# TensorE reads the normalised columns themselves, and SyncE reads two tile places at its block's start

## What is computed

```python
def _L1_ffn_ref(x, ln1_w, ln1_b, w_qkv, w_proj, ln2_w, ln2_b, gate_w, gate_b, w1, w2):
    ...
    x = x + _msa(_layernorm(x, ln1_w, ln1_b), w_qkv, w_proj)     # 16 heads of 8 columns, softmax attention within a batch
    x = x + _moe_mlp(_layernorm(x, ln2_w, ln2_b), gate_w, gate_b, w1, w2)   # each row goes to 1 of 8 experts, 128 -> 512 -> 128
    return x
```

## Time and profile before

| | |
|---|---|
| runs | 586.36 to 586.48 us, median 586.46 |
| profiled execution | 586.56 us, its span 584.8 us |
| mean granted TensorE clock | 0.944 |
| busy: TensorE, VectorE, ScalarE, GpSimd | 504.4, 357.7, 283.5, 152.5 us |
| attention block | 375.8 to 496.2 us of the span |
| expert block | 496.3 us to the end |

### The profile page before, as it was taken

One profiled execution on the slowest core, in us unless ns is written; L12 is line 12 of the kernel. 1 busy time (PEld: TensorE's weight loads), 2 busy tenths in 40 slices (PEclk: granted clock), 3 DMA queues, 4 the chain that ended last, 5 costly groups with the idle time before them and its releaser, 6 DMA issues. The chain is left out here.

```text
span 584.8 us, 33765 instructions
## 1 busy us (share of the span) xinstructions
PE 504.4 (86%) x14446; PEld 411.1 (70%) x14446; DVE 357.7 (61%) x1202; ACT 283.5 (48%) x691; POOL 152.5 (26%) x270
## 2 busy tenths in 40 slices
PE   0799999999996999899999979689999970799995
PEld 0688888888885654566666658468888850799994
DVE  4655555555556666566666446557999985355552
ACT  4222222221221694455555544558887851577772
POOL 2111111111110000000000017543467665155553
PEclk9899999999998999999999998669999995799998
DMA  8060000000000027494230002000011112333430
GB/s 272 23 233 1 0 0 0 0 0 0 0 0 2 0 41 162 132 321 75 73 92 0 2 2 76 1 4 1 0 58 39 58 66 91 80 111 101 111 106 18
DMA packets 22653, 34.36 MB, mean 59 GB/s; under 512 B 3616, under 2 KB 15909, under 8 KB 22216
## 3 DMA queue, kind: packets, MB, share of 16 engines
q1 hardware_dynamic: 19824, 27.23, 16.8%
q0 software_dynamic: 2784, 6.56, 3.2%
HBM read 25.98 MB, written 8.26 MB: 59 GB/s over the span
## 5 line engine op out<-in xcount | busy, mean ns | idle before, releaser
L231 PEld LDWEIGHTS ps_u<-v_cur,buf_b 128*32 128x32 f32 x7936 | 78.6, 110 | 12.1 <-DVE v_cur L300 9.4
L231 PE MATMUL ps_u<-v_cur,buf_b 128*32 128x32 f32 x7936 | 82.5, 198 | 3.7 <-DVE buf_b L289 2.4
L215 PE MATMUL ps_v<-buf_a,u_pad 128*32 128x128 f32 x1984 | 68.5, 280 | 7.5 <-issue 6.1
L215 PEld LDWEIGHTS ps_v<-buf_a,u_pad 128*32 128x32 f32 x1984 | 53.1, 112 | 11.1 <-issue 9.4
L300 DVE RECIPROCAL v_cur<-ps_vt 128x32 f32<-128x32 f32 x124 | 35.3, 327 | 32.3 <-PE ps_vt L222 32.3
L593 PE MATMUL ps_h<-buf_c,up 128*128 128x512 f32 x96 | 50.8, 626 | 0.4 <-DVE buf_c L809 0.2
L1735 POOL DMA_INDIRECT out<-yb,token_i x39 | 38.4, 984 | 48.2 <-DVE resid L1837 47.1
L179 POOL TENSOR_TENSOR u_hist<-inv_u,r_sum 128x16 f32 x62 | 13.8, 223 | 132.2 <-DVE inv_u L307 132.2
L985 POOL MEMSET eps<- 128x1 f32 x1 | 0.1, 99 | 166.4 <-POOLq L526 166.4
L1758 PE MATMUL m_h<-xT,w_near 128*128 128x128 f32 x312 | 43.0, 283 | 0.0
L195 ACT ACTIVATE over<-u_diff 128x32 f32<-128x32 f32 x31 | 7.1, 230 | 72.4 <-POOL u_diff L175 72.4
(11 more groups left out here) (309 smaller groups left out, 1133.8 us busy)
## 6 DMA issues: line engine op xcount, KB each, us to landing
cw_b<-cw_d SPq DMA_DIRECT2D x16, 512.0 KB, 8.1
xt<-sorted_x SPq DMA_DIRECT2D x39, 136.0 KB
w<-in_w SPq DMA_DIRECT2D x2, 2048.0 KB, 16.4
buf_a<-in_x SPq DMA_DIRECT2D x4, 512.0 KB, 6.4
buf_b<-in_x_t SPq DMA_DIRECT2D x4, 512.0 KB, 6.8
buf_d<-in_x_nt SPq DMA_DIRECT2D x1, 2048.0 KB, 9.9
sorted_x<-nobody SPq DMA_DIRECT2D x1, 1088.0 KB, 4.6
out<-yb,token_i POOLq DMA_INDIRECT x39
```

Of the source, the lines that this page charges most:

```text
L215: last = mm(ps_v[h][32 * j:32 * j + 32, 0:D], u_pad[:, h, j, 32 * i4:32 * i4 + 32], K[:, g * D:(g + 1) * D], start=i4 == 0, stop=i4 == TI - 1)
L231: last = mm(rows_u[h][32 * q:32 * q + 32, g, :], KT[:, b * N:(b + 1) * N], v_cur[:, h, k:k + 1].broadcast_to([P, WIDE]), start=True, stop= ...
```

## The change

The buffers `xs`, their copies and the semaphore `x_in` go. TensorE's three projection matmuls of a chunk read `xn_t`; within the loop their operand's address is worked out from the loop's register. In the expert block SyncE reads the places of tiles 0 and 1 before its two waits, and from the third tile on it reads as before.

```diff
-        xs = mem.sb("xs", [P, 2, CB, N])
...
-                g.tensor_copy(xs[:, 0], xn_t[:, 0:CB, :]).then_inc(x_in, 1)
-
...
-                def chunk_in(k):
-                    if k >= 2:
-                        pool.wait_ge(v_mm, k - 1)
-                    g.tensor_copy(xs[:, k % 2], xn_t[:, k * CB:(k + 1) * CB, :]).then_inc(x_in, 1)
-
-                chunk_in(1)
...
-                    if c + 2 < NC:
-                        chunk_in(c + 2)
...
-                def project(c, k):
-                    pe.wait_ge(x_in, c + 1)
+                def batches_of(c):
+                    return xn_t[:, c * CB:(c + 1) * CB, :] if isinstance(c, int) else xn_t[:, bass.ds(c * CB, CB), :]
+
+                def project(c):
                     if past(c, 1):
                         pe.wait_ge(qk_out, c)
-                    mm(ps_qk[:, 0, :], w_qkv[:, 0, :], xs[:, k], start=True, stop=True)
-                    mm(ps_qk[:, 1, :], w_qkv[:, 1, :], xs[:, k], start=True, stop=True).then_inc(qk_mm, 1)
+                    mm(ps_qk[:, 0, :], w_qkv[:, 0, :], batches_of(c), start=True, stop=True)
+                    mm(ps_qk[:, 1, :], w_qkv[:, 1, :], batches_of(c), start=True, stop=True).then_inc(qk_mm, 1)
...
-                    mm(ps_v[:, 0:CT], w_qkv[:, 2, :], xs[:, k], start=True, stop=True).then_inc(v_mm, 1)
+                    mm(ps_v[:, 0:CT], w_qkv[:, 2, :], batches_of(c), start=True, stop=True).then_inc(v_mm, 1)
...
             def _(sp):
+                first = [sp.value_load(tables.base_i[0:1, d:d + 1], min_val=0, max_val=SLOTS - P) for d in range(2)]
                 sp.wait_ge(tables.sent, 16 * N)
                 sp.wait_ge(tables.filled, 16)
                 for d in range(TILES):
                     k = d % BUFS
-                    at = sp.value_load(tables.base_i[0:1, d:d + 1], min_val=0, max_val=SLOTS - P)
+                    at = first[d] if d < 2 else sp.value_load(tables.base_i[0:1, d:d + 1], min_val=0, max_val=SLOTS - P)
```

More of the change, by code:

```diff
@@ L1269, in attend_and_route @@
         names = ("qk_mm", "v_mm", "s_mm", "t_mm", "o_mm", "ot_mm", "p_mm", "r_mm",
-                 "qk_out", "exp_done", "t_out", "ot_out", "x_in", "rooted", "act_own",
+                 "qk_out", "exp_done", "t_out", "ot_out", "rooted", "act_own",
                  "max_done", "sub_done", "v_out", "on_done", "x2_done", "summed", "row_ends", "hot_done", "slots_done",
                  "own", "heads", "v_read", "scoring")
-        (qk_mm, v_mm, s_mm, t_mm, o_mm, ot_mm, p_mm, r_mm, qk_out, exp_done, t_out, ot_out, x_in,
+        (qk_mm, v_mm, s_mm, t_mm, o_mm, ot_mm, p_mm, r_mm, qk_out, exp_done, t_out, ot_out,
          rooted, act_own, max_done, sub_done, v_out, on_done, x2_done, summed, row_ends, hot_done, slots_done,
@@ L1335, in past, with values @@
                     return not isinstance(c, int) or c >= n
-                def project(c, k):
-                    pe.wait_ge(x_in, c + 1)
+                def batches_of(c):
+                    return xn_t[:, c * CB:(c + 1) * CB, :] if isinstance(c, int) else xn_t[:, bass.ds(c * CB, CB), :]
+                def project(c):
                     if past(c, 1):
                         pe.wait_ge(qk_out, c)
-                    mm(ps_qk[:, 0, :], w_qkv[:, 0, :], xs[:, k], start=True, stop=True)
-                    mm(ps_qk[:, 1, :], w_qkv[:, 1, :], xs[:, k], start=True, stop=True).then_inc(qk_mm, 1)
-                def values(c, k):
+                    mm(ps_qk[:, 0, :], w_qkv[:, 0, :], batches_of(c), start=True, stop=True)
+                    mm(ps_qk[:, 1, :], w_qkv[:, 1, :], batches_of(c), start=True, stop=True).then_inc(qk_mm, 1)
+                def values(c):
                     if past(c, 1):
@@ L1433, in body @@
                     if not isinstance(c, int) or c + 1 < NC:
-                        project(c + 1, 1 - k)
-                        values(c + 1, 1 - k)
+                        project(c + 1)
+                        values(c + 1)
                     if past(c, 2):
@@ L1442, in _ @@
                 pe.wait_ge(made, RANKS)
-                project(0, 0)
-                values(0, 0)
+                project(0)
+                values(0)
                 body(0, 0, 0)
```

## The result

The changed kernel takes 580.93 us (median of 15 executions, 578.75 to 584.10), the kernel before 584.89 (15 executions beside them, 581.80 to 586.73). The ratio is **0.9937 [0.9918, 0.9956]**: faster by 0.6%, where the forecast was 586.1 and "no change that can be told". The same kernel on two other chips gave 0.9951 [0.9923, 0.9979] and 0.9937 [0.9911, 0.9963]. The profiled execution after is 579.32 us, its span 577.6 and its mean granted clock 0.957; before it was 586.56, 584.8 and 0.944.

The account below looks back on a forecast made before the run. Bounds: GpSimd's copy at the start, VectorE in late pairs, GpSimd's sends at the tail, TensorE in the experts. 0.21 + 0.71 less 0.26 leaves 0.66, half kept: 586.46 - 0.33 = 586.1 us; range 585.0 to 587.3.

Parts of the forecast that it names:

- The first copy goes: -0.21: Start of the attention block: TensorE starts 0.42 us earlier without GpSimd's copy of chunk 0, of which 0.21 us stays.
- The halving: Attention start: if the clock's rise keeps its time, 0.42 us more of low clock does the work of 0.21.
- The odd chunks' collisions: -0.71: Late loop pairs: copies slow VectorE's L1602 by 0.24 us, for which TensorE waits; three such copies go, 0.71 us less.
- rival C: No effect: collisions are coincidence, the start is bound by fetching, SyncE's 0.26 is halved; 586.6 us, chance 0.14.
- GpSimd's sends also slow VectorE a little; they stay: Late pairs, L1590: a slowdown put down to GpSimd's sends, which the change keeps, so no gain was counted.
- The even chunks: 0: Late pairs: 0.18 us freed at L1582 is lost as VectorE's reciprocal waits for TensorE's mixing; 0, at most 0.56.
- TensorE's operand: 0: Loop projections: register operations for the address are covered by the sequencer's lead of 0.9 to 1.2 us; bounds 0 and 7.2.
- rival B: Slower: address registers in the loop's three projection calls per chunk starve the array; up to 591.7 us, chance 0.10.
- SyncE: +0.26: Hand-over to the experts: the second read now delays tile 0's DMA, first expert matmul 0.26 us later; bounds -0.1, +0.7.
- Half is kept in the experts: -0.33: Experts' start: 0.66 us earlier, but at half speed up to a clock rise that keeps its time, so 0.33 remains.
- Rival A: More is kept: the even chunks' 0.56 counts too, the rises move with the work, nothing halved; 585.0 us, chance 0.18.
- Its neighbour at 585.8: Between forecast and 585.0: the clock's rises move, the even chunks give nothing; counted with the forecast, together 0.55.

Follow-up runs that it names:

- e7: The kernel before, but TensorE reads chunk 0 in place; the copies of chunks 1 to 15 stay: 582.39 us, ratio 0.9979 to the kernel before.
- e8: The changed kernel once more, same source, on another chip: 580.97 us, ratio 0.9951 to the kernel before.
- e3: The changed kernel with GpSimd's sixteen copies put back at their old places, into a tile nobody reads: 582.79 us, ratio 0.9977 to the kernel before.
- e4: The changed kernel with sixteen copies nobody reads, each issued ahead of its chunk's two sends instead of behind: 580.84 us, ratio 0.9945 to the kernel before.
- e12: The changed kernel, but the loop's projections all read chunk 0's columns, with no computed address; one execution, pairs of 11.76, 11.43, 11.47, 11.47 and 11.44 us.

## Why the prediction was wrong

Between the forecast, 586.1, and the measured median, 580.93, lie 5.2 us. 2.1 of them are the base (586.46 against a mean of 584.40), 2.7 the gain (3.06 in the mean against 0.33), and 0.4 the distance of this median from the changed kernel's mean.

The mean went down by 3.06 us. The stages that the change touches give 1.85 of it (profiles with the copies against those without): start 0.36; the third, fourth and fifth pair 0.17, 0.42 and 0.45; the sixth pair, in the tail, 0.46; the sends 0.11; less 0.12 for SyncE (0.08 to 0.20, by which profiles are compared). Outside the span there are 0.69. Some 0.5 us are left, which the clock could hold (mean granted clock 0.950 before and 0.953 after), and which is no more than the means can tell.

*The first copy goes: -0.21.* The copy was what TensorE waited for, and 0.36 us of the 0.42 came. The halving failed: the clock's rise did not keep its time. It stood 13.5 us behind the barrier in the profile read, and at 3.2 in that of after; but e7, with the other copies in place, has it at 3.3, and e8, the changed kernel, at 7.6. The prediction had named this as what would make it fall. The difference between the two profiles is in part luck and no proof of the change.

*The odd chunks' collisions: -0.71.* The mechanism held, for the copies and no coincidence (e3 brings all back), which shuts out rival C. Its "for it", that the operations are slow for the sends' sake, is right only for the 0.07 us where a send starts. The term was mis-sized. The step that failed is "GpSimd's sends also slow VectorE a little; they stay". The slow L1590 that it names did not stay: its 0.16 us was the queued copy's doing (e4) and went with the copy. In e3 two of these pairs lose some 0.07 more, and the third 0.03, to a send that starts beside an operation; in the kernel after none starts there. So each pair gave 0.42 to 0.46 instead of 0.24; and one more pair, the third of the loop, gave 0.17 where nothing was counted: in e3 its L1605 takes 0.34 us ahead of a queued copy, 0.15 more than at best. That is 1.50 for four pairs against 0.71.

*The even chunks: 0.* Right: L1573 is short again, and the reciprocal waits 0.18 us for the mixing.

*TensorE's operand: 0.* Right, and rival B with it is out: one register operation and 0.9 us of lead (e12). The forecast's three operations per chunk were one.

*SyncE: +0.26.* Right in sign and place, and twice too large. The first DMA slipped from 5.09 to 5.62 us behind the last send, the second moved from 6.25 to 6.21, and the first expert matmul slipped 0.11 us. The read that came ahead took 0.28 us in the chain, as the earlier trace rows had it, where the Trainium skill (DMA: Bandwidth & Descriptors, Latency and other measured facts) gives a floor of about 600 ns; the measurement decides.

*Half is kept in the experts: -0.33.* Failed as a rule. The rise there lay 5.2 us behind the first transposition in the profile of before, and from 3.5 to 7.4 in the others, with 83.9 to 86.4 us from that transposition to the end. This is a spread of 2.5 us that no edit here is shown to steer, against a halving of 0.66.

*Nothing outside the span, and the base.* The sum carried 1.8 us around the span over unchanged; the mean of before is 2.42. And it set its range, 2.3 us wide, around 586.46, though three executions so near each other said nothing of the spread: of the kernel before's own 155 executions 93 fell below 585.0, the range's lower end. The largest fault was this: a forecast for a median of many had the width of one profile's arithmetic. Rival A (585.0) had the right direction, but its even chunks gave nothing. Its neighbour at 585.8 frees one of the two halvings only; with both, as it is worded, the sum gives 585.6.

The Trainium skill (SBUF — State Buffer, Who interferes with whom) has a VectorE instruction with two SBUF inputs contend with a GpSimd instruction that reads SBUF. The runs agree on the copy and on the memset, which reads nothing. That VectorE's operation is slow already in the send ahead of a queued copy is not in the rule, and is some 0.6 of the 1.50 us won.

## What to carry to other kernels

Before GpSimd's work is called free because GpSimd idles, look at which VectorE operations run beside it, the instruction ahead of it in its queue included; either take the reading work away or put it where VectorE has a long operation from PSUM, which was worth as much here. A read that is moved ahead of waits gains only if those waits last: here they took 0.02 us, and the moved read delayed the first transfer by half a microsecond. And ask for the spread of the kernel before ahead of giving a range: where the clock's rises move by microseconds from one execution to the next, one profile places a rise, but not the kernel's.

## What the hardware showed that was not expected

- An operation of VectorE with two operands from SBUF that began 0.30 to 0.56 us behind the start of GpSimd's indirect DMA lost 0.065 to 0.24 us if a copy that reads SBUF stood next in GpSimd's queue (35 cases), and 0.014 at most if none did (292 cases).
- Of the operations in whose first 0.05 us such a DMA started 47 of 62 lost 0.04 to 0.08 us, with a copy behind it or without: 0.212 us against 0.161 in the kernel after.
- Eight recorded waits more at the end of TensorE's program took the time outside the span from 2.42 us in the mean to 1.70.
- From the first projection to the first rank matmul the same work took 11.6, 12.5, 13.9 or 15.3 us, by whether TensorE's clock rose before the barrier or 3.1 to 4.0, 7.6 or 13.5 us behind it. The changed kernel's own three profiles have 12.5, 13.9 and 12.5.
